# A ring of four buffers instead of seven for gathered node rows in a graph-network kernel

## The reference

```python
def _genconv(h, edge_attr, src, dst, w1, b1, g1, bb1, w2, b2, t):
    msg = relu(h[src] + edge_attr) + EPS_MSG          # 100000 x 64
    m = msg * t
    ex = exp(m - segment_max(m, dst)[dst])
    alpha = ex / (segment_sum(ex, dst)[dst] + 1e-16)
    agg = segment_sum(msg * alpha, dst)               # 3125 x 64
    z = relu(_layernorm((h + agg) @ w1 + b1, g1, bb1))
    return z @ w2 + b2

h = x @ enc_node_w + enc_node_b
e = edge_attr @ enc_edge_w + enc_edge_b
h = _genconv(h, e, ...)                               # layer 1
for i in range(1, 4):                                 # layers 2 to 4
    z = relu(_layernorm(h, ln_g[i], ln_b[i]))
    h = h + _genconv(z, e, ...)
```

## Time and profile before

| | |
|---|---|
| median of three runs | 5210.84 us |
| the profiled execution, its own time | 5190.08 us |
| its span, first to last instruction | 5188.3 us |
| PE busy | 2437.5 us, 47% |
| DVE busy | 2861.0 us, 55% |
| ACT busy | 1751.9 us, 34% |
| POOL busy | 3104.2 us, 60% |
| DMA, mean | 98 GB/s |
| granted TensorE clock, mean | 0.643 of full speed |

### The profile page before, as it was taken

The page is one execution under the profiler, slowest core; times in us unless marked ns, Lnnn a source line. Parts: engine busy times, 40 slices in busy tenths (PEclk is TensorE's granted clock), DMA queues, the critical chain, the costliest instruction groups (busy, mean ns, idle before and its releaser), DMA issues.

```text
span 5188.3 us, 36882 instructions
## 1 busy us (share of the span) xinstructions
PE 2437.5 (47%) x9731; PEld 1698.6 (33%) x9731; DVE 2861.0 (55%) x3666; ACT 1751.9 (34%) x3407; POOL 3104.2 (60%) x3248
## 2 busy tenths in 40 slices
PE   2465666655434444444433444444452444444454
PEld 2354444443323232333222322333231333323233
DVE  3476666766335555555534555555551555555565
ACT  1333333334223333333323333333341333333333
POOL 4666666663566666666356666666626666666651
PEclk8556655667556666666656666666655666666665
DMA  2344444444123333333213333333321333333332
GB/s 62 94 124 122 123 117 118 123 119 148 40 76 102 102 105 100 104 106 100 90 39 92 96 105 105 98 108 102 100 73 40 104 106 99 104 97 104 98 105 68
DMA packets 369056, 508.17 MB, mean 98 GB/s; under 512 B 171775, under 2 KB 177657, under 8 KB 368828
## 3 DMA queue, kind: packets, MB, share of 16 engines
q1 hardware_dynamic: 262222, 395.37, 23.8%
q0 software_dynamic: 103552, 109.52, 10.4%
q10 hardware_dynamic: 3054, 0.71, 0.1%
HBM read 217.93 MB, written 287.39 MB: 97 GB/s over the span
## 4 chain that ended last, share of the span: by engine, by line
another core or an unknown queue 40%; ACT 20%; issue 19%; DVE 10%; PE 9%; DMA 1%; POOL 1%; DVEq 0%; ACTq 0%; SPq 0%; POOLq 0%
ACT sw_out L604 6%; PE pT L782 5%; ACT r L589 3%; DVE S L1096 3%; ACT decay L596 3%; DVE W L1100 2%; ACT pX L592 2%; ACT u L591 2%; ACT pX L598 2%; DVE pX L1098 1%; PE pX L766 1%; PE pX L771 1%; ACT pA L592 1%; DVE M L1081 1%
## 5 line engine op out<-in xcount | busy, mean ns | idle before, releaser
L511 POOL DMA_INDIRECT zsrc<-z_rows,idx_all x3136 | 3007.7, 959 | 1745.2 <-issue 981.0
L782 PE MATMUL pT<-ident,S 128*128 128x128 f32 x1568 | 606.2, 396 | 2255.3 <-DVE W L1100 1307.1
L604 ACT ACTIVATE sw_out<-pT 128x512 f32<-128x512 f32 x784 | 424.9, 594 | 2603.2 <-remote 1798.0
L782 PEld LDWEIGHTS pT<-ident,S 128*128 128x128 f32 x1568 | 338.2, 216 | 2349.5 <-issue 2208.3
L1096 DVE TENSOR_TENSOR_SCAN S<-decay,S,pX 128x512 f32<-128x512 f32 x296 | 378.3, 1278 | 1099.6 <-ACT decay L596 678.4
L766 PE MATMUL pX<-attr_pair,edge_w 128*128 128x512 f32 x592 | 563.0, 1051 | 141.9 <-issue 75.1
L771 PEld LDWEIGHTS pX<-ident,zsrc 128*128 128x128 f32 x2368 | 479.5, 281 | 355.1 <-issue 264.9
L782 PE MATMUL pT<-ident,W 128*128 128x128 f32 x1568 | 579.2, 379 | 0.0
L1081 DVE TENSOR_TENSOR_SCAN M<-pR,M,u 128x512 f32<-128x512 f32 x296 | 376.5, 1272 | 317.4 <-ACT u L591 240.1
L771 PE MATMUL pX<-ident,zsrc 128*128 128x128 f32 x2368 | 460.7, 360 | 75.5 <-DMA zsrc<-z_rows,idx_all 75.5
L1096 DVE TENSOR_TENSOR_SCAN S<-decay,S,pA 128x512 f32<-128x512 f32 x96 | 122.9, 1280 | 635.9 <-ACT decay L596 386.8
(11 more groups left out here) (189 smaller groups left out, 3166.3 us busy)
## 6 DMA issues: line engine op xcount, KB each, us to landing
sw_rows<-sw_out SPq DMA_DIRECT2D x392, 512.0 KB
attr_pair<-attr_cols SPq DMA_DIRECT2D x153, 512.0 KB
zsrc<-z_rows,idx_all POOLq DMA_INDIRECT x3136
max_cols<-M SPq DMA_DIRECT2D x196, 256.0 KB
attr_in<-in_edge_attr_dram SPq DMA_DIRECT2D x196, 128.0 KB
attr_cols<-attr_pair SPq DMA_DIRECT2D x49, 512.0 KB
z_rows<-z SPq DMA_DIRECT2D x25, 125.0 KB
node_sw<-sw_rows,row_idx POOLq DMA_INDIRECT x100
```

Source lines behind the costliest of these rows:

```text
L511: pool.indirect_dma_start(zsrc[c % RING][:, t4, h, :], None, z_rows, bass.IndirectOffsetOnAxis(idx_all[:, h, t4, c:c + 1].bitcast(U32), 0) ...
L604: act.activation(sw_out[c % 2][:, :, 2 * b:2 * b + 2, :, :].rearrange("p h t s c -> p (t s) h c"), pT[b][:, :].rearrange("p (a h c) -> p a ...
L782: last = pe.transpose(pT[b][:, at:at + P], scanned[c % 2][:, t4:CH:SUB], ident[:, :])
```

## The change

The ring of gathered rows gets four buffers in place of seven. 98 is not a multiple of 4, so the number of uses is kept for each buffer (25 for buffers 0 and 1, 24 for 2 and 3), and PE's wait takes the count of its own buffer. POOL's wait follows from `RING`: block c now waits for the matmuls of chunk c - 4.

```diff
-RING = 7
-USES = NCH // RING
-assert USES * RING == NCH
+RING = 4
+USES = [len(range(b, NCH, RING)) for b in range(RING)]
...
                 def add_nodes(c):
-                    pe.wait_ge(gathered[c % RING], value(pe, l * (128 * USES)) + 128 * (c // RING + 1))
+                    pe.wait_ge(gathered[c % RING], value(pe, l * (128 * USES[c % RING])) + 128 * (c // RING + 1))
```

## The result

The median after the change is 5124.4 us (5118.39 to 5129.46, four runs) against 5210.02; the ratio is 0.9833 with a 95% interval of [0.9821, 0.9846]. The forecast was 5146 within 5100 to 5235, and faster with a chance of 0.62. The profiled execution takes 5121.75 us (span 5119.9).

What follows compares the result with a forecast made beforehand. POOL's gathers were taken to hold back PE's reports until POOL stops at a full ring. The start's -115 and the end's +50 gave -65 us, from the median 5210.84 to 5146, range 5100 to 5235.

Steps and rivals of the forecast that it cites:

- PE's reports are held beside POOL's gathers, and a shorter distance stops POOL sooner: Node matmuls and turns back: reports come 3 to 4 us after POOL stops, which it does only when the ring is full.
- rival B: Layer start: PE's lateness is its own, chunk 3's nodes stay at +111; slower, 5261 us; chance 0.24 together with D.
- (c): Steady stretch: the cycle of 34.2 us for three chunks stays; about 20 us of cover left, late rows cost nothing.
- (d): Layer start: block 6 at +63 to +73, block 7 at about +83 us after block 0, reports earlier; 115 us gained.
- (e): Layer end: three chunks more at the steady pace, three fewer at 7.5 us; 12 us a layer, 13 in layer 1, taken as +50.
- The sign named for it: Layer end in the profile after: block 97 to the last scan 53 us in place of 64.9.
- Sum: Whole kernel: -115 + 50 = -65 us, from the median 5210.84 to 5146 us.
- The reason I gave in short: Three blocks leave the layer start, where 30 us of gathers stall PE, and go where 34 us of them carry three chunks.
- Rival C: Start and later stretch: PE's fixed catching up goes only when POOL is idle, gain and loss cancel near 5211; chance 0.14.
- Rival D: PE's waits for gathered rows: cover shrinks, ten waits of 3 us a layer, +120, 5266 with A's gain; folded into B.

Runs made afterwards that it cites:

- e1: Kernel before with its seven buffers kept, but block c waits for the matmuls of chunk c - 4: 5107.2 us, ratio 0.9837.
- e11: Changed kernel with each gather replaced by POOL's plain copy of 128 adjacent rows, on a chip where PE's reports come late under gathers: 3452.1 us.
- e2: Kernel before with seven buffers, blocks 0 to 9 of a layer waiting for chunk c - 4, later ones for c - 7: 5193.1 us, ratio 1.001.
- e10: Kernel before with distance 4 only from block 85 of a layer on, on a chip where PE's reports come late: 5191.5 us, ratio 0.9993.
- e5: Kernel before with distance 4 only from block 85 of a layer on, on a quick chip: 4370.3 us, ratio 0.9998.

## Why the prediction was right, step by step

- **PE's reports are held beside POOL's gathers, and a shorter distance stops POOL sooner:** right in the main. e1 shows that the wait alone does it, e11 that without gathers by index the lateness is gone. "Held back until POOL stops" is too strong: in layer 2 of before chunk 2's nodes (+63.2) and the turn back of chunk 0 (+85.6) were reported while POOL issued without a pause, and chunk 2's came no earlier with the stop. PE is slowed under gathers and not blocked. The rule that rival B took from the Trainium skill, "SBUF — State Buffer", section "SBUF: two separate sides", would have given 5261; the run went the other way. The section speaks of the ports to SBUF, and no run shows that a port is what makes PE late. What does is not shown.
- **(c) the steady pace stays, rows are in time:** right. 11.4 and 11.6 us a chunk; the node matmuls' waits for rows 75.5 and 74.0 us in the largest groups. The cover, put at 20 us, was larger than needed: even a ring of two, with none, kept the pace.
- **(d) the start, -115 us:** block 7 came at +79.4, +80.1, +80.1 and +80.1 where the prediction had +83, which makes 127.7 us and not 115. In layers 3 and 4 it came as told: block 6 at +61.8 and +60.7, and block 7 after waits of 8.6 and 9.7 us. In layer 2 block 6 came at +66.6 and block 7's own wait was 3.9 us; in layer 1 POOL stood 8.0 us before block 6 and not at all before block 7. Block 7 lies at +80 all the same.
- **(e) the end, +50 us:** 57 measured. Between the block that waits for chunk 3's nodes (10 before, 7 after) and block 97 it is +147 for the four layers, 33.4, 34.3 and 32.4 in layers 2 to 4, where the prediction had 34.3, and 47.2 in layer 1, where it had 36. From block 97 to the last scan it is -90, in the mean 22.5 a layer, just what three chunks at 7.5 us give. The term was right in kind and 7 us too small, all of it in layer 1. The sign named for it was wrong, though: block 97 to the last scan was to be "53 us", which takes off the net 12 in place of the 22.5; 64.9 - 22.5 is 42.4, and 42.2 was measured.
- **Sum:** -70 for the four layers by the profiles, forecast -65. Both terms were too small, (d) by 13 and (e) by 7, and they have opposite signs, so the nearness of the sum is in part luck. The medians give -86; most of the 16 us between are the profiled execution of before, which lay 20 us below its median.
- **The reason I gave in short,** that three blocks leave the start, "where 30 us of gathers let PE do next to nothing", was too narrow, and e2 shows it: the same three blocks cost as much when they come after block 9. The cost is that of each block of lead: about 10 us in which PE gets next to nothing done when the lead is built up, of which the tail gives back only some 4 us (a chunk there takes 7.4 in place of 11.4). That is an estimate of 6 us less for each buffer and layer: 6 x 3 x 4 = 72 us for this change (70 by the profiles, 86 by the medians, 80 in e1), 96 for three buffers (112 measured) and 120 for two (116).
- **Rival C, no change,** described e2 and e10 well, where the distance is cut for part of a layer, and the change not at all. **Rival B** fell: chunk 3's nodes were reported at +79, not at +111. **Rival D** fell: late rows cost nothing measurable even with two buffers.
- **What the prediction could not know:** all of it holds for one kind of chip. Where the kernel before takes 5187 to 5210 us PE is held; on two chips (4371 us) it isn't, and there the distance decided nothing. The result fell on the kind of chip that the trace came from. On the other kind the forecast of a gain would have been wrong, and nothing in the rows of before could tell.

## What to carry to other kernels

A buffer ring between a producer that sets the pace and a consumer that keeps up needs only the depth that covers the time from issue to landing. If the producer also disturbs the consumer while it runs ahead, each further buffer is lead that is paid for once a layer (10 us here) and given back only in part (4 us). Cut the distance throughout: at the start only, or at the end only, it gave nothing. And where waits end "remote" on a single core, run the kernel on a second chip before explaining them: here the chip made 16%, and the change 1.7%.

## What the runs showed of the hardware

The same program has medians of 5187.0, 5192.8 and 5210.0 us in three of the comparisons and 4371.3 and 4370.8 us on the two quick chips. On the first kind PE's reports come late while POOL issues gathers by index: chunk 3's nodes in layer 2 have their last matmul's recorded end at 1405.6 and are reported at 1473.2, 68 us later and 11 us after POOL stopped; in the steady stretch the copy starts 3 to 4 us after POOL stops. On the second kind reports are on time (391 of 392 within 0.02 us of the recorded end in e5). With plain copies from POOL, 544 ns each in place of 958, reports are on time in every chunk on either kind, and the pace is 7.46 us. PE's busy time is nearly the same in both (2437.5 in before, 2461.2 us in e5), but the ends of matmuls are modelled, so this doesn't tell whether the array itself is slower under gathers. The granted clock was 0.643 and 0.676 on average. Why chips differ so stays open.
